# Output projection spread over most units of an attention group, and value pages issued by the sync engine

## The reference

```python
x = x + einsum('bct,bcd->bdt', x, W0[cond])             # L0: mixes the 32 rows, by condition
x = x + x @ base_weight.T + bias + lora(x, adapter_ids) # L1
# L2: attention of 32 new tokens over 16 cached pages of 32 tokens and themselves
q, k, v = x @ Wq.T, x @ Wk.T, x @ Wv.T                  # 32 query heads, 8 key and value heads, 128 wide
q, k = rope(rmsnorm(q)), rope(rmsnorm(k))
kc, vc = k_cache[block_table], v_cache[block_table]     # (64, 512, 8, 128) each
probs = softmax(q @ [kc, k].T / sqrt(128), masked by cache_seqlens)
x = x + (probs @ [vc, v]) @ Wo.T
x = x + einsum('bct,bcd->bdt', x, W3[cond])             # L3
```

## Time and profile before

| | |
|---|---|
| time of the three runs | 2388.29, 2390.04, 2393.2 us |
| the profiled execution's own time | 2394.14 us |
| its span | 2392.4 us |
| granted TensorE clock, mean | 0.994 |
| busy, share of the span | TensorE 97%, VectorE 74%, ScalarE 64%, GpSimd 58% |
| stages: L0 and L1; projections; attention; end | 0 to about 105; to about 730; to about 2191; to 2392 us |

### The profile page before, as it was taken

The page is one execution under the profiler, slowest core; times in us unless marked ns, Lnnn a source line. Parts: engine busy times, 40 slices in busy tenths (PEclk is TensorE's granted clock), DMA queues, the critical chain, the costliest instruction groups (busy, mean ns, idle before and its releaser), DMA issues.

```text
span 2392.4 us, 58277 instructions
## 1 busy us (share of the span) xinstructions
PE 2312.0 (97%) x15392; PEld 2010.2 (84%) x15392; DVE 1760.8 (74%) x5422; ACT 1535.2 (64%) x4221; POOL 1395.5 (58%) x2249
## 2 busy tenths in 40 slices
PE   8999999999998899999999999999999999998999
PEld 5778888888887788888888888888888888887777
DVE  4434777777778887887887887887887887886232
ACT  4324666666667777777777777777777777775221
POOL 1003454444447777877877877877877877872000
PEclk9999999999998999999999999999999999999999
DMA  4335333333337777777767777777767777775332
GB/s 164 95 110 163 102 98 102 111 106 102 97 115 257 221 224 239 253 228 237 255 223 241 253 228 237 255 223 242 252 220 245 253 223 241 253 221 194 110 132 101
DMA packets 347959, 455.96 MB, mean 191 GB/s; under 512 B 34506, under 2 KB 280842, under 8 KB 343695
## 3 DMA queue, kind: packets, MB, share of 16 engines
q1 hardware_dynamic: 308398, 315.83, 41.9%
q0 software_dynamic: 36864, 134.23, 16.9%
q10 hardware_dynamic: 2528, 4.29, 0.5%
HBM read 374.53 MB, written 79.69 MB: 190 GB/s over the span
## 4 chain that ended last, share of the span: by engine, by line
PE 48%; DVE 23%; issue 19%; ACT 5%; POOL 3%; DMA 1%; DVEq 0%; ACTq 0%; POOLq 0%; SPq 0%
PE S L1168 11%; PE oP L1168 11%; DVE regC L987 8%; PE S L1260 7%; DVE k_lo L284 7%; PE oP L1241 3%; PE oP L1092 3%; DVE regC L986 3%; PE S L1209 3%; PE bank L1092 2%; PE oP L1122 2%; ACT regC L721 2%; PE bank L1260 2%; DVE nmx L975 1%; DVE rinv L981 1%
## 5 line engine op out<-in xcount | busy, mean ns | idle before, releaser
L1241 PE MATMUL oP<-regC,regK 128*128 128x128 f32 x4096 | 541.2, 275 | 0.1
L1241 PEld LDWEIGHTS oP<-regC,regK 128*128 128x128 f32 x4096 | 507.2, 192 | 9.6 <-issue 0.3
L975 DVE CUSTOM_DVE_ANT_0 regC<-S,mask 128x544 f32<-128x544 f32 x512 | 368.1, 719 | 187.9 <-issue 185.7
L715 ACT CAST k_hi<-regK 128x544 fp32r<-128x544 f32 x512 | 331.3, 647 | 210.5 <-PE S L1209 184.1
L721 ACT ACTIVATE regC<-regC,nmx 128x544 f32<-128x544 f32 x512 | 384.9, 752 | 58.8 <-DVE nmx L975 49.8
L534 POOL TENSOR_TENSOR regC<-regC 128x256 f32<-128x256 f32 x320 | 244.3, 784 | 278.3 <-DVE regC L944 278.3
L549 POOL TENSOR_TENSOR q_hi<-regC,ones 128x128 fp32r<-128x128 f32 x512 | 262.3, 512 | 233.8 <-PE S L1209 229.1
L1092 PE MATMUL bank<-ident,regC 128*128 128x128 f32 x2048 | 321.1, 279 | 26.9 <-ACT regC L765 21.0
L284 POOL TENSOR_TENSOR k_lo<-regK,k_hi 128x192 fp32r<-128x192 f32 x512 | 341.4, 667 | 3.3 <-ACT k_hi L715 3.3
L987 DVE TENSOR_SCALAR regC<-regC,rinv 128x512 f32<-128x512 f32 x512 | 337.8, 660 | 0.0
L284 DVE TENSOR_TENSOR k_lo<-regK,k_hi 128x352 fp32r<-128x352 f32 x512 | 328.2, 641 | 2.9 <-ACT k_hi L715 2.9
(11 more groups left out here) (137 smaller groups left out, 4468.9 us busy)
## 6 DMA issues: line engine op xcount, KB each, us to landing
regK<-kT_cache SPq DMA_DIRECT2D x1024, 128.0 KB
qkT_d<-regC SPq DMA_DIRECT2D x160, 256.0 KB, 2.3
regC<-qkT_d SPq DMA_DIRECT2D x64, 512.0 KB
oT_d<-regC SPq DMA_DIRECT2D x64, 256.0 KB
regK<-oT_d SPq DMA_DIRECT2D x16, 1024.0 KB, 5.0
regC<-wqk SPq DMA_DIRECT2D x10, 1024.0 KB, 5.2
v_d<-regC SPq DMA_DIRECT2D x32, 256.0 KB, 2.3
regK<-qkT_d SPq DMA_DIRECT2D x64, 128.0 KB
```

What stands on the lines that cost most here:

```text
L715: nc.scalar.copy(k_hi[u % 2].rearrange("p (s t) -> p s t", t=PSIZE), k_sb[b][:, :, h, :]).then_inc(s_khi, 1)
L975: nc.vector.tensor_tensor_reduce(out=p_sb[u % 4], in0=scores, in1=mask[u // HK % 2][:], scale=-SCALE, scalar=3e38, op0=ALU.add, op1=ALU.mi ...
L1241: last = nc.tensor.matmul(oP[:, j * 512:j * 512 + P], v_sb[b][:, m, u % HK * D:(u % HK + 1) * D], pT_sb[u % 2][:, m * P:(m + 1) * P], star ...
```

## The change

Four things are edited together.

1. **The projection's 48 matmuls are dealt out singly.** `WO_AT` now gives a number of matmuls for each unit: two at units 30, 31 and 0 to 19, three at units 0, 6, 10 and 14. `residual` moves from unit 6 to unit 20.
2. **`oT_hi` and `oT_lo` get six slots of one batch each** (`SLOTS`, `slot_of`) where there were four, so that the next tile's first two batches can be written while the projection still reads. Tiles of even number use slots 0 to 3, odd ones 4, 5, 2, 3; the odd tiles' rows are therefore rotated, and the load and store of their `x2_d` rows is done in two DMAs of 64 rows. The wait for `s_wo` moves from a tile's first batch to its third. Since the slots depend on the tile's parity, every engine's loop body now holds two groups.
3. **Value pages are loaded by SyncE**: `load_v_pages` issues 16 DMAs of one page (32 rows of 4 KB) for each batch, from the page numbers that `load_pages` already holds in registers, after the wait for `s_po`. For batch 0 they stand between its key pages and the first store of the projections, for batch 1 after its own values.
4. **The gathers, index copies and index computation go away** from GpSimd and VectorE.

```diff
-WO_AT = {UG - 2: 0, UG - 1: 2, 0: 4, 1: 6, 2: 8, 3: 11, 4: 14, 5: H2}
+SLOTS = 6
+WO_AT = {u: 3 if u in (0, 6, 10, 14) else 2 for u in (UG - 2, UG - 1, *range(20))}
...
+        def slot_of(o, par, b):
+
+            k = 4 + b if par and b < 2 else b
+            return o.rearrange("p (j r n) -> p j r n", j=4, n=SLOTS * C)[:, :, :, k * C:(k + 1) * C]
...
+            def load_v_pages(pages, par, first=0):
+
+                for n in range(first, first + len(pages)):
+                    sp.dma_start(v_sb[par][n % 4 * PSIZE:(n % 4 + 1) * PSIZE, n // 4, :],
+                                 v_cache[bass.ds(pages[n - first], 1)].rearrange("a t n -> (a t) n")).then_inc(s_v[par], 16)
...
-            load_pages(0, 0)
+            load_v_pages(load_pages(0, 0), 0)
...
             load_own(1, 1)
             load_own_v(1, 1)
+            for i in range(8):
+                load_v_pages(pages1[i], 1, i * 2)
...
-                        load_pages(b, k % 2)
+                        pages = load_pages(b, k % 2)
                         sp.wait_ge(s_po, g * (2 * BT) + 2 * (k + 1))
+                        load_v_pages(pages, k % 2)
                         load_own_v(b, k % 2)
...
-                    if k == 0 and not first:
+                    if k == 2 and not first:
                         sp.wait_ge(s_x2y, g)
-                        sp.dma_start(x2_d[bass.ds(g - 1, 1)].rearrange("a p n -> p (a n)"), x2r).then_inc(s_x2yst, 16)
-                    if k == 1:
-                        ge(sp, s_x2yst, g * 16)
-                        sp.dma_start(x2r, x2_d[bass.ds(g, 1)].rearrange("a p n -> p (a n)")).then_inc(s_x2r, 16)
+                        store_rows(g - 1, 1 - par)
+                    if k == 3:
+                        ge(sp, s_x2yst, g * 32)
+                        load_rows(g, par)
...
-            def gather_v(k, par, m):
-                nc.gpsimd.indirect_dma_start(
-                    out=v_sb[par][:, m, :], out_offset=None, in_=v_cache,
-                    in_offset=bass.IndirectOffsetOnAxis(ap=idx[k][:, m:m + 1], axis=0)).then_inc(s_v[par], 16)
...
-                    if q == 0:
+                    b = q // 2
+                    if b == 2:
                         ge(act, s_wo, g)
...
-                for h in range(h0, h1):
-                    last = split_product(yP, (oT_hi, oT_lo), (wo_hi, wo_lo), h, h == 0, h == H2 - 1)
-                if h1 == H2:
+                for i in range(first, first + count):
+                    h, (a, w) = i // 3, ((oT_hi, wo_hi), (oT_hi, wo_lo), (oT_lo, wo_hi))[i % 3]
+                    at = (h * SLOTS + (2 if par else 0)) * C
+                    last = nc.tensor.matmul(yP, a[:, at:at + P], w[:, h * T:(h + 1) * T],
+                                            start=(i == 0), stop=(i == 3 * H2 - 1))
+                if first + count == 3 * H2:
                     last.then_inc(s_wo, 1)
```

More of the change, by code:

```diff
@@ L50 @@
 H2 = HQ // 2
-WO_AT = {UG - 2: 0, UG - 1: 2, 0: 4, 1: 6, 2: 8, 3: 11, 4: 14, 5: H2}
+SLOTS = 6
+WO_AT = {u: 3 if u in (0, 6, 10, 14) else 2 for u in (UG - 2, UG - 1, *range(20))}
+WO_FROM, at = {}, 0
+for u in WO_AT:
+    WO_FROM[u], at = at, at + WO_AT[u]
+assert at == 3 * H2
+WO_END = 20
 LOW = 11
@@ L407, in _, with rows_of, load_rows, store_rows @@
             sp.dma_start(wo_raw, wo[0]).then_inc(s_wo_in, 16)
-            def group(g, first, last):
+            def rows_of(g, par):
+                for i in range(2):
+                    a = (1 - i if par else i) * 2 * C
+                    yield x2r[i * 2 * C:(i + 1) * 2 * C, :], x2_d[bass.ds(g, 1), a:a + 2 * C].rearrange("a p n -> p (a n)")
+            def load_rows(g, par):
+                for here, there in rows_of(g, par):
+                    sp.dma_start(here, there).then_inc(s_x2r, 16)
+            def store_rows(g, par):
+                for here, there in rows_of(g, par):
+                    sp.dma_start(there, here).then_inc(s_x2yst, 16)
+            def group(g, par, first, last):
                 for k in range(BT):
@@ L749, in split_wo, with step @@
                 nc.scalar.copy(wo_hi[:, at], raw[:, at]).then_inc(s_wohi, 1)
[L751 removed]
+            def step(g, u, par):
                 n = g * UG + u
@@ L784, in _, with group @@
             for u in range(ROT):
-                step(0, u)
+                step(0, u, 0)
                 if 0 <= u - WO_SPLIT < H2:
                     split_wo(0, u - WO_SPLIT, wo_raw)
-            with act.Fori(0, NT - 1) as g:
+            def group(g, par):
                 for u in range(ROT, UG):
-                    step(g, u)
+                    step(g, u, par)
                 for u in range(ROT):
-                    step(g + 1, u)
+                    step(g + 1, u, 1 - par)
+            with act.Fori(0, NT // 2 - 1) as gg:
+                group(gg * 2, 0)
+                group(gg * 2 + 1, 1)
+            group(NT - 2, 0)
             for u in range(ROT, UG):
-                step(NT - 1, u)
+                step(NT - 1, u, 1)
             own_turned(NT - 1, UG)
-            out_heads(NT - 1, UG)
+            out_heads(NT - 1, UG, 1)
             def high(g, i):
@@ L1005, in split_wo, with step @@
                 nc.vector.tensor_tensor(lo[:, at], raw[:, at], wo_hi[:, at].bitcast(F32), ALU.subtract).then_inc(s_wolo, 1)
-            def step(g, u, before):
+            def step(g, u, before, par):
                 n = g * UG + u
@@ L1020, in step @@
                 if u % HK == 4:
-                    out_low(g, u // HK)
-                if before is not None and u == 6:
+                    out_low(g, u // HK, par)
+                if before is not None and u == WO_END:
                     residual(before)
@@ L1042, in _, with group @@
                         dve.wait_ge(s_qst[j], 16 * QKB * NT // 2)
-                step(0, u, None)
+                step(0, u, None, 0)
                 if 0 <= u - WO_SPLIT < H2:
                     split_wo(0, u - WO_SPLIT, wo_lo, wo_raw)
-            with dve.Fori(0, NT - 1) as g:
+            def group(g, par):
                 for u in range(ROT, UG):
-                    step(g, u, None)
+                    step(g, u, None, par)
                 for u in range(ROT):
-                    step(g + 1, u, g)
+                    step(g + 1, u, g, 1 - par)
+            with dve.Fori(0, NT // 2 - 1) as gg:
+                group(gg * 2, 0)
+                group(gg * 2 + 1, 1)
+            group(NT - 2, 0)
             for u in range(ROT, UG):
-                step(NT - 1, u, None)
+                step(NT - 1, u, None, 1)
             def low(g, i):
@@ L1261, in split_product, with out_proj, step @@
                 return done
-            def out_proj(g, h0, h1):
-                if h0 == 0:
+            def out_proj(g, par, first, count):
+                if first == 0:
                     pe.wait_ge(s_oev, g * BT + BT)
                     pe.wait_ge(s_wolo, H2)
-                for h in range(h0, h1):
-                    last = split_product(yP, (oT_hi, oT_lo), (wo_hi, wo_lo), h, h == 0, h == H2 - 1)
-                if h1 == H2:
+                for i in range(first, first + count):
[4 more added lines that the diff above has]
+                if first + count == 3 * H2:
                     last.then_inc(s_wo, 1)
-            def step(g, u, before):
+            def step(g, u, before, par):
                 n = g * UG + u
@@ L1283, in step @@
                 of = g if u >= UG - 2 else before
-                if u in WO_AT and WO_AT[u] < H2 and of is not None:
-                    out_proj(of, WO_AT[u], WO_AT[(u + 1) % UG])
+                if u in WO_AT and of is not None:
+                    out_proj(of, par if of is g else 1 - par, WO_FROM[u], WO_AT[u])
                 if u > 0:
```

105 lines of the change are left out of this document (39 added, 66 removed).

## The result

| | before | changed |
|---|---|---|
| median of four runs each | 2389.59 us | 2669.88 us (2668.43 to 2673.59) |
| ratio | 1 | 1.117, 95% interval 1.115 to 1.119 |
| the profiled execution's own time, its span | 2394.14, 2392.4 us | 2668.43, 2666.7 us |
| mean granted TensorE clock | 0.994 | 0.949 |

The kernel is 11.7% slower. The forecast was 2614 us, and 2540 to 2680 as its range: the sign, the mechanism and the range held, the point was 56 us too low. (The median of the kernel before is 2390.04 us for the three runs given further up; here a fourth is in it.)

The account below looks back on a forecast made before the run. SyncE's issue queue, 1153 of 1382.9 us busy, was to become the bound in place of TensorE: 2394.1 + 5.5 (value pages of batch 0) + 215 (attention, 1598 against 1382.9) = 2614 us, range 2540 to 2680.

Parts of the forecast that it names:

- The signs named beforehand: In attention: no SyncE waits on `s_qp`, 16 value pages in 7 to 8 us, 26 us a batch, TensorE about 90% busy.
- value pages: SyncE in attention: 16 more DMAs in each of 61 batches at 0.46 us, 449 us of issue against 230 of waiting.
- rows of x2_d in 64-row DMAs: SyncE in attention: one load and one store more for each of 15 groups, 30 x 0.5 = 15 us.
- ends of SyncE's loop: SyncE in attention: 14 loop ends become 7, each branch 2.8 us, so 19 us less.
- the loop of two groups: Attention loops: 19 us less on SyncE, nothing on other engines, since no group showed a step that TensorE's 90.00 us would not hide.
- Prologue: Before attention: batch 0's sixteen value DMAs delay the projections' first store to 236.5 us, costing 5.5 us.
- The end: After the last loaded batch: 12 units and the last projection stay, eight matmuls move to the end at the same cost, 0.
- Gathers and dealing out: Attention: removing gathers counts 0; dealing out covers 3.4 us a group, 53 us in all, hidden under SyncE's issue, so 0.
- Cheaper issue: SyncE in attention: value pages issue at 0.30 us like single rows, 156 us less, 2458 us; chance 0.11.
- the faster case: Attention: SyncE hides the pages in its idle time and TensorE's waits are covered, 2347 us; chance 0.03.
- the dearer one: SyncE in attention: the pages' issue is held back to 0.60 us, 137 us more, 2751 us; chance 0.10 together with the falling clock.
- The falling clock: TensorE's clock falls in each batch's pause: no effect if short, 2780 us if low for most of a batch; 0.10 with the dearer one.

Follow-up runs that it names:

- e_v8: Changed kernel with the value pages in 8 DMAs of 64 rows a batch instead of 16, same bytes, other pages read; 2518.02 us, one run.
- e_v4: Changed kernel with the value pages in 4 DMAs of 128 rows a batch, same bytes, other pages read; 2378.89 us, 0.996 of the kernel before.
- e_nochk: Changed kernel without the run-time bounds test of page numbers, 32 register instructions fewer a batch on SyncE; 2437.14 us.
- e_loop2: Kernel before, with only TensorE's attention loop running over two groups instead of one, same matmuls in the same order; 2406.36 us.
- e_vsp: Kernel before with value pages loaded by SyncE instead of gathers; loops of one group, no dealing out, rows in one DMA; 2602.14 us.
- e_vsp2: Kernel before with value pages loaded by SyncE instead of gathers, and TensorE's attention loop over two groups; no dealing out; 2657.59 us.
- e_deal_u: Changed kernel with values by GpSimd's gathers again and the attention loops of SyncE, ScalarE, VectorE and TensorE written out without a branch; 2337.72 us.
- e_deal: Changed kernel with the value pages taken back to GpSimd's gathers, keeping dealing out and six slots; 2374.67 us, 0.9935 of the kernel before.

## Why the prediction was right, and where it was off

*What bounds the kernel.* Right. The argument was that a queue which computes nothing was 1153 of 1382.9 us busy, and that 449 do not fit into 230. SyncE's waits went from 230 to 4 us, ScalarE's split now waits for the key pages' DMA, and three edits that change only what SyncE has to do (e_v8, e_v4, e_nochk) moved the time by about what they took off the queue, 148, 340 and 250 us for 152, 291 and 233: in e_v4 the computing kept the rest, in e_nochk the other lines of the queue grew. The signs named beforehand came out so: 16 value pages in 7.3 to 8 us in 51 of 62 batches, up to 9.1 in the others; TensorE busy 89%; the first store of the projections at 236.62, forecast 236.5; a period of 27.1 us where 26 was named.

*The terms, in the 61 periods.* Forecast 1598 us, measured 1655.5. The table gives SyncE's time by line, from one instruction's start to the next one's, without waits.

| term | forecast | measured | off by |
|---|---|---|---|
| value pages | +449 (0.46 each) | +472.5 (0.484) | +24 |
| key pages, own keys and queries, own values, store | as before, 766 | 796 | +30 |
| rows of x2_d in 64-row DMAs | +15 | 42.0 - 17.0 = +25 | +10 |
| registers | as before, 322 | 316 | -6 |
| ends of SyncE's loop | -19 | 36.0 to 18.1 = -18 | +1 |

*The step that failed* is in the part on the loop of two groups: "I leave this at nothing on the other engines". It is not nothing there. TensorE's longer loop costs 16 us in the kernel before, and 55 in the kernel that SyncE bounds, where SyncE's issues get longer as its code is fetched. That is a cost which an engine far from the bound lays on the one that is the bound, and no term of the sum could hold it. In the changed kernel the prolonged issues have 69 us in excess, in the kernel before, whose times the forecast carried on, 9: those 60 us are about the 57.5 by which the 61 periods exceeded the forecast. In the table they are spread over the lines that issue. The reason given, that none of the groups before showed such a step, was no reason: before, no loop was that long. The Trainium skill (Runtime: NRT & Kernel Launch, Instruction fetch mechanics) says that straight code is fetched ahead, that a taken branch out of the pages held forces a fetch before execution goes on, and that TensorE's memory holds 2,048 instructions. The trace agrees: 90 us of attention in e_loop2 (1400 to 1490 us), about one group, hold 698 matmuls and 697 weight loads, so a loop over one group would fit by that figure, as an estimate, and one over two not, and writing the loops out took the waits away. That another engine's DMA issues get longer with the fetches rests on the runs alone.

*Sizes.* A DMA of 64 rows of x2_d was taken at 0.5 us and measured about 0.7 with what surrounds it. The value page at 0.46, from the own values' row, the nearest in shape, was nearly right: 0.478 where little code is fetched (e_vsp), and 0.484 in the changed kernel. Some of that is luck, since the price does not follow the shape evenly: with 64 rows a DMA it would have been 0.666. For e_vsp the terms of the forecast would have given 2394.1 + 5.5 + 1153 + 449 - 1382.9 = 2619 and it took 2602, since key pages issued in 519.7 us instead of 539.3 and registers took 9 us less, while the value pages took 466.2 instead of 449; why key pages were quicker there is open. The point was thus 17 too high for the value pages on SyncE taken by themselves, and too low by more than that in the term left out.

*Prologue.* The store of the first projection came out where it was forecast; of the 5.5 us, 4.3 were found at batch 2's first issue. *The end:* forecast unchanged, measured 2.6 us less. The loop's ends taken as 14 and 7 are 13 and 6 (a loop's last pass has no branch back); the difference, 7, is the same.

*Gathers and dealing out.* Both were priced at nothing under SyncE's issue, and that held: with the dealing out or without it (the changed kernel and e_vsp2), the times are 12 us apart, and other terms account for it. What the dealing out is worth where TensorE is the bound was put at 3.4 us a group and 53 in all: in e_deal_u a group went from 90.0 to 86.6, and the kernel gained 52. That gain came with the gathers in place, and e_v4, which has none, runs its shorter groups in 86.7 us where e_deal with them has 87.0. So the rule of the Trainium skill on starved descriptors, weighed in the prediction, had next to nothing to give here. A gather took in e_deal_u what it took before:

```profile
L533 POOL DMA_INDIRECT regK<-v_cache,idx x256: 941/984/1965, 198.1 to 2102.4; - x128
```

*The rivals.* Cheaper issue (0.30) and the faster case (0.23 and under) fall: 0.484. So does the dearer one (0.60), and e_v4 moves the same bytes in 2379 us. The falling clock did happen, and without effect, as the prediction's own sum had it. The windows view of 104 us, nearly one group (us; busy and count of TensorE, its weight loads, VectorE, ScalarE, GpSimd; granted clock; share of the DMA engines; GB/s) beside the earlier trace rows:

```profile
1516.00:1620.00 104.00, 86.12 (x649) 80.21 (x648) 71.53 (x218) 62.94 (x135) 45.21 (x90) 0.91 0.72 200
```

and in steps of 6 us, around the pause shown in the section on the result:

```profile
1552.00:1558.00 6.00, 6.00 (x50) 5.75 (x48) 5.66 (x19) 4.01 (x9) 2.94 (x6) 1.00 0.65 201
1558.00:1564.00 6.00, 2.84 (x29) 2.48 (x28) 2.77 (x8) 3.18 (x7) 3.08 (x6) 1.00 0.85 256
1564.00:1570.00 6.00, 6.00 (x41) 5.98 (x40) 4.71 (x17) 4.02 (x9) 2.37 (x6) 0.72 0.79 210
1570.00:1576.00 6.00, 5.91 (x53) 5.36 (x52) 5.66 (x17) 5.33 (x12) 3.61 (x8) 1.00 0.43 130
```

TensorE was busy 2.84 of 6 us, and in the 6 us after that the granted clock was 0.72 on average, between its two levels of 1.2 and 2.4 GHz; then it was back. That costs nothing here: TensorE waits again at the next batch, and SyncE, which sets the pace, waits 4 us in all.

## What to carry to other kernels

A queue that only issues has a budget like an engine: add up its instructions, registers and tests among them, against the time the others give it, and before moving work onto it ask what it can drop. Here four wide DMAs in place of sixteen, or leaving out the bounds tests, was worth 291 and 233 us (the wide DMAs need pages that lie side by side in the cache, which the block table does not give), and leaving the gathers where they were was worth more than either. A loop made longer so that buffers can alternate has a price of its own at its branch and in the fetched code: compare it once with the same code written out.

## What the runs showed of the hardware

- The issue of one DMA from SyncE lasts longer for 64 rows (545 ns in the median, 483 at least) than for 32 (370, 315) or for 128 (381, 332), at 4 KB a row in each. I had expected one price. Why it is so is open.
- With TensorE's longer loop, DMA issues of SyncE that fall together with packets of instruction queue 8 last longer, by 0.8 us on average: 9 prolonged issues with 12 packets in that stretch (e_vsp), 81 with 99 (e_vsp2). Whether issues of ScalarE or GpSimd suffer as well is open.
- A backward branch over two groups of attention cost TensorE 2.8 and 3.5 us (16.5 us in 6 waits in e_loop2, 20.9 in 6 in e_deal), one over a single group nothing that the waits of the kernel before show; about as much straight code cost nothing that the waits show either (e_deal_u), though 108 packets were fetched.
- Testing one page number against a bound is 0.25 us of SyncE's time; with 16 a batch it was 4.1 of 27.1 us.
